# Cross-attention: context and K halves in two buffers each, projections in another order of steps, later weights asked for in the last group but one

## The reference

```python
x = x + xattn(layernorm(x), ctx, Wq, Wk, Wv, Wo)   # 16 heads of 16, ctx 32 x 256 x 256, no mask, no scale
x = x + attn(layernorm(x), wq, wk, wv, wo)         # 16 heads of 64, causal
x = x + ffn(layernorm(x), ...)                     # 256 -> 1024 -> 256, exact gelu, int8 weights, int16 activations
# xattn: q, k, v = split_heads(x @ Wq, ctx @ Wk, ctx @ Wv); softmax(q k^T) v; @ Wo
```

## Time and profile before

| | us |
|---|---|
| median of 3 runs | 672.53 |
| lowest and highest run | 670.81, 673.95 |
| span of the profiled execution | 669.4 |
| PE (matmul) busy | 608.3 (91%) |
| VectorE (DVE), ScalarE (ACT), GpSimd (POOL) busy | 469.9, 388.8, 197.3 |

### The profile page before, as it was taken

The page is one execution under the profiler, slowest core; times in us unless marked ns, Lnnn a source line. Parts: engine busy times, 40 slices in busy tenths (PEclk is TensorE's granted clock), DMA queues, the critical chain, the costliest instruction groups (busy, mean ns, idle before and its releaser), DMA issues. The chain is left out here.

```text
span 669.4 us, 18523 instructions
## 1 busy us (share of the span) xinstructions
PE 608.3 (91%) x6772; PEld 520.5 (78%) x6796; DVE 469.9 (70%) x989; ACT 388.8 (58%) x1017; POOL 197.3 (29%) x308
## 2 busy tenths in 40 slices
PE   6788799999999899979998999999999999788997
PEld 3577788888989788865887898888888897644597
DVE  4376867878787677875789847575756656467797
ACT  3386767888888687874351515242424333357895
POOL 4736234545454544400020303030312111250000
PEclk9899989999999899999999999999999999899999
DMA  7888958585857586720300000000000000000012
GB/s 252 184 236 215 269 143 208 139 211 139 210 136 186 117 199 146 171 52 3 125 2 1 2 1 0 0 0 0 0 0 0 2 1 2 9 3 0 1 43 84
DMA packets 35597, 58.44 MB, mean 87 GB/s; under 512 B 6912, under 2 KB 15232, under 8 KB 35552
## 3 DMA queue, kind: packets, MB, share of 16 engines
q1 hardware_dynamic: 25008, 36.85, 21.8%
q0 software_dynamic: 5952, 12.20, 7.5%
q10 hardware_dynamic: 4592, 8.78, 4.8%
HBM read 17.96 MB, written 2.10 MB: 30 GB/s over the span
## 5 line engine op out<-in xcount | busy, mean ns | idle before, releaser
L573 ACT ACTIVATE Pr<-pS,nmax 128x256 f32<-128x256 f32 x256 | 119.8, 480 | 25.1 <-DVE nmax L677 24.5
L677 DVE TENSOR_REDUCE nmax<-pS 128x2 f32<-128x512 f32 x128 | 87.4, 683 | 35.6 <-PE pS L416 35.2
L899 POOL TENSOR_TENSOR a_Pr<-a_Pr,a_rinv 128x512 f32<-128x512 f32 x32 | 32.8, 1045 | 185.8 <-DVE a_rinv L1188 185.8
L426 PE MATMUL pT<-ident,Pr 128*128 128x128 f32 x512 | 78.5, 276 | 0.1
L416 PE MATMUL pS<-Kst,Qst 96*128 96x256 f32 x256 | 57.2, 305 | 21.6 <-DMA Kst<-KSl 16.6
L341 POOL TENSOR_TENSOR CSl<-CT,CSh 128x1024 fp32r<-128x1024 f32 x15 | 35.3, 2355 | 114.5 <-ACT CSh L566 114.5
L271 POOL DMA_DIRECT2D Qst<-QSh x124 | 62.0, 503 | 13.7 <-DVE QSl L649 6.9
L416 PEld LDWEIGHTS pS<-Kst,Qst 96*128 96x128 f32 x256 | 41.5, 192 | 30.2 <-issue 15.2
L1068 ACT ACTIVATE a_Pr<-a_Pr 128x512 f32<-128x512 f32 x32 | 20.2, 631 | 76.0 <-DVE a_Pr L1180 76.0
L426 PEld LDWEIGHTS pT<-ident,Pr 128*128 128x128 f32 x512 | 60.1, 142 | 0.8 <-ACT Pr L573 0.4
L573 ACT ACTIVATION_READ_ACCUMULATOR Pr<-pS,nmax 128x1 f32 x256 | 54.1, 211 | 0.0
(11 more groups left out here) (269 smaller groups left out, 1925.1 us busy)
## 6 DMA issues: line engine op xcount, KB each, us to landing
Kst<-KSh SPq DMA_DIRECT2D x126, 128.0 KB, 2.9
CT<-ctxT ACTq DMA_DIRECT2D x16, 512.0 KB, 5.6
Kst<-KSl SPq DMA_DIRECT2D x63, 128.0 KB, 3.7
Qst<-QSh POOLq DMA_DIRECT2D x124, 64.0 KB, 2.1
Qst<-QSl POOLq DMA_DIRECT2D x62, 64.0 KB, 2.1
X<-x SPq DMA_DIRECT2D x4, 512.0 KB, 9.0
out<-X SPq DMA_DIRECT2D x8, 256.0 KB, 2.2
raw<-awq SPq DMA_DIRECT2D x1, 1024.0 KB, 5.9
```

The lines of the kernel that those rows point to most:

```text
L426: last = pe.transpose(pT[s % 2][:, t, k, :], Pr[s % 2][:, t, P * k:P * k + P], ident[:, :])
L573: act.activation(Pr[c % 2][:, t, :], pS[c % 2][:, t, :], ACT.Exp, bias=nmax[c % 2][:, t:t + 1], accum_out=rsum[par][:, c // 4, 2 * (c % 4) ...
L677: dve.tensor_reduce(nmax[s % 2][:, :], pS[s % 2][:, :, :], AX.X, ALU.max, negate=True).then_inc(maxed, 1)
L899: pool.tensor_tensor(rows, rows, rinv[s][:, :].unsqueeze(2).to_broadcast([P, 8, SQ]), ALU.mult).then_inc(weighted, 1)
```

## The change

It has five parts. `CS` gets two buffers by the pair's parity. `KS` gets two as well; the second lies in the tensor WO_ints, which the third layer fills later. In the table of events, K of the next even pair moves from steps 6 and 7 to 2 and 3, V of this odd pair from 2 and 3 to 6 and 7, V of the next even pair from 9 and 10 to 10 and 14, and K of the next odd pair from 13 and 14 to 11 and 12. ScalarE's `ctx_high` and `load_ctx` move with it. Before the first group, K of pair 1 comes ahead of the first two scores, with 10 and 4 spare matmuls for 22 and 12. The self-attention's weights are asked for in group 6.

```diff
-        CS = [sb(f"CS{s}", [P, KC, PK], F32R) for s in "hl"]
+        CS = [[sb(f"CS{b}{s}", [P, KC, PK], F32R) for s in "hl"] for b in range(2)]
...
-        KS = [sb(f"KS{s}", [P, 2, PK], F32R) for s in "hl"]
+        KS = [[sb(f"KS{s}", [P, 2, PK], F32R) for s in "hl"],
+              [ints[:, 4 * s:4 * s + 4, :].rearrange("p (a b) d -> p a (b d)", a=2) for s in range(2)]]
...
+        EVENTS = {0: (0, "X", 2, 0), 2: (1, "K", 2, 0), 3: (2, "K", 2, 1), 4: (3, "Q", 2, 0), 6: (4, "V", 1, 0),
+                  7: (5, "V", 1, 1), 10: (6, "V", 2, 0), 11: (7, "K", 3, 0), 12: (8, "K", 3, 1), 14: (9, "V", 2, 1)}
...
             def body(i, last):
-                p = 2 * i
-                first = isinstance(i, int) and i == 0
+                late = isinstance(i, int) and i == QUADS - 2
                 if not last:
-                    if first:
+                    restack_k(sp, 0, EV0 + EV * i + 2, CHUNKS * (2 * i + 1))
+                    if late:
                         load_later(0)
-                    restack_k(sp, 0, EV0 + EV * i + 5, CHUNKS * (p + 1))
-                    if first:
-                        load_later(1)
-                        load_later(2)
-                    restack_k(sp, 1, EV0 + EV * i + 9, CHUNKS * (p + 2))
-                    if first:
-                        load_later(3)
+                    restack_k(sp, 1, EV0 + EV * i + 8, CHUNKS * (2 * i + 2))
+                    if late:
+                        for m in range(1, 4):
+                            load_later(m)
...
-            spare(22)
+            spare(10)
             for r, (kind, ahead, part) in enumerate(AHEAD):
...
-                if r == 6:
-                    spare(12)
-                    score(0, 0)
-                    score(0, 1)
-                project(r, r, kind, part, ahead, 3)
+                project(r, r, kind, part, ahead, ahead % 2, 3)
+            spare(4)
+            score(0, 0)
+            score(0, 1)
...
             for r, (kind, ahead, part) in enumerate(AHEAD):
-                if r == 6:
-                    ctx_high(1, 1, 6)
-                    exps(0, 0)
                 high(r, r, kind, ahead, part, None)
                 if r == 2:
                     restack_k(act, 0, 1, 0, (3,))
+                    ctx_high(1, 1, 0)
+                    load_ctx(2, 0, 1)
+            load_ctx(3, 1, 2)
+            exps(0, 0)
+            ctx_high(0, 2, 6)
...
-                    if s == 0 and not last:
-                        load_ctx(2 * i + 2, 0, 2 * i + 1)
-                    if s == 2 and not last:
-                        load_ctx(2 * i + 3, 1, 2 * i + 2)
+                    if s == 3 and two_ahead(i):
+                        load_ctx(2 * i + 4, 0, 2 * i + 3)
+                    if s == 13 and two_ahead(i):
+                        load_ctx(2 * i + 5, 1, 2 * i + 4)
...
-                    if s == 4 and not last:
-                        ctx_high(0, i + 2, EV0 + EV * i + 3)
-                    if s == 11 and not last:
-                        ctx_high(1, i + 2, EV0 + EV * i + 8)
+                    if s == 8 and not last:
+                        ctx_high(1, i + 2, EV0 + EV * i + 6)
+                    if s == 15 and two_ahead(i):
+                        ctx_high(0, i + 3, EV0 + EV * i + 10)
```

More of the change, by code:

```diff
@@ L377, in weights, with project @@
                 return [(W[HI][:, m, k, cols], W[LO][:, m, k, cols]) for k in range(KC)]
-            def project(r, k_, kind, part, pair, q_needs=None):
+            def project(r, k_, kind, part, pair, b, q_needs=None):
                 after(pe, lo, r - 1)
@@ L396, in project @@
                     pe.wait_ge(ctx_lo, pair + 1)
-                    last = split_matmul(pe, bank[:, :], weights(1, slice(P * part, P * part + P)), parts(CS))
+                    last = split_matmul(pe, bank[:, :], weights(1, slice(P * part, P * part + P)), parts(CS[b]))
                 else:
@@ L437, in weigh @@
                     first = isinstance(i, int) and i == 0
-                    pe.wait_ge(lo, EV0 + EV * i + (2 if last else 3) if par else 6 if first else EV0 + EV * i - 2)
+                    pe.wait_ge(lo, EV0 + EV * i + (2 if last else 6) if par else 6 if first else EV0 + EV * i)
                     after(pe, merged, 2 * i + par)
@@ L494, in body @@
                         r, k, kind, ahead, part = event(i, s, last)
-                        project(r, k, kind, part, 2 * i + ahead, r - 1)
+                        project(r, k, kind, part, 2 * i + ahead, ahead % 2, r - 1)
                     if s == 11 or (s == 3 and not first):
@@ L559, in high @@
                 else:
-                    dst, how, kw = target(HI, kind, part)
+                    dst, how, kw = target(HI, kind, part, ahead % 2)
                     act.activation(dst, bank[:, :].rearrange(how, **kw) if kw else bank[:, :], ACT.Copy).then_inc(hi, 1)
@@ L653, in low @@
                 else:
-                    dst, how, kw = target(LO, kind, part)
-                    high = f32(target(HI, kind, part)[0])
+                    dst, how, kw = target(LO, kind, part, ahead % 2)
+                    high = f32(target(HI, kind, part, ahead % 2)[0])
                     dve.tensor_tensor(dst, bank[:, :].rearrange(how, **kw) if kw else bank[:, :], high,
```

30 lines of the change are left out of this document (13 added, 17 removed).

## The result

| | before | after |
|---|---|---|
| median of 4 runs each, us (same chip) | 672.25 | 661.44 (659.37 to 661.87) |
| ratio, 95% interval | | 0.9837, 0.9804 to 0.9871 |
| profiled execution: span, us | 669.4 | 657.6 |
| its own time, us | | 659.37 |
| cross-attention ends (first `a_pO` matmul), us | 311.38 | 299.89 |

The kernel is 1.6% faster. The forecast was 658 us in a range of 649 to 667, with 0.85 on faster. Sign and size were right, and so was the mechanism of the gain, the waits for Kst and `On`; the new limit that it named, GpSimd at step 11, hardly shows. The median is 3.4 us above the forecast, half a per cent. One term of the sum, group 5, was further off than that, by 3.9 us, and the steady groups were 1.9 us off the other way; the two partly cancel.

The account below looks back on a forecast made before the run. TensorE was taken to set the pace, its idle time being what groups can give back. Span 669.4 - 17.4 (groups) + 3.4 (start) = 655.4 us, plus 3.1 from span to median: 658 us, range 649 to 667.

Parts of the forecast that it names:

- Waits for Kst: Cross-attention scores at steps 6 and 14: earlier K projections remove the waits, 16.6 us in ten before.
- cover of 3.8 us: Kst[1] restack: landed 40.2 us after the group's start, wanted at 44.0, so 3.8 us to spare.
- rival 3: Q and Kst[1] restacks collide with a context load from 28 to 37 us into each group: 662 us, chance 0.08.
- `On` and the weights: Step 12's wait for `On` is covered, 0.83 us less a group; moving the later weights to group 6 costed at 0.
- Steady group: A cross-attention group without its Kst wait: 32.45 us, less 0.83 for `On`, plus 1.3 of new waiting, 32.9 us.
- wait of 1.3 us for CSl at step 11: TensorE's K projection waits 1.3 us for GpSimd's low context part, seen 22.6 us into the group; bounds 0 and 3.
- Rival 2: CSl is ready in time at step 11, so the 1.3 us wait is gone in seven groups: 649 us, chance 0.11.
- group 5 4.1: Group 5, 36.97 us with a 2.96 us Kst wait and slow clock, was to give back 4.1 us.
- nothing to spare: CSl at step 2: GpSimd needs 8.35 us of some 8.5 available; no wait, costed at 0, 0.3 a group for range.
- Rival 4: Slower than before: the CSl wait nears 3 us and the clock falls in each of seven groups: 681 us, chance 0.09.
- The start: Before group 0: K of pair 1 ahead of the scores puts the third score at 36.1 us for 32.80; 3.4 lost.
- Rival 1: TensorE's clock stays low into group 0, 5 us of work at half rate: +2.5, 661 us, chance 0.18.

Follow-up runs that it names:

- Experiment 4: The changed kernel with one KS instead of two, K of each parity waiting for the other restack: 686.12 us, ratio 1.0228 to the kernel before.
- experiment 1: The kernel before with only the four later weights' loads moved from group 0 to group 6: 665.71 us, ratio 0.9908.
- experiment 2: The changed kernel with the later weights asked for in group 0 again: 659.73 us, ratio 0.9832 to the kernel before.
- experiment 8: The changed kernel with nine of the twelve DMAs of each Qst[0] restack on SyncE, GpSimd issuing 123: 653.66 us, ratio 0.9755 to the kernel before.
- experiment 12: The changed kernel with nine DMAs per Qst[0] restack on SyncE and the old start, pair 2's context load kept early: 652.5 us, ratio 0.9710.
- experiment 5: The changed kernel with the old start (22 and 12 spare matmuls, first two scores ahead of K of pair 1): 657.81 us, ratio 0.9802.
- experiment 10: The changed kernel with nine DMAs per Qst[0] restack on SyncE and the old start, pair 2's context load beside the Q restack: 654.74 us, 0.9740.
- experiment 3: The changed kernel with 20 more spare matmuls ahead of K of pair 1 at the start: 656.30 us, ratio 0.9762 to the kernel before.
- experiment 9: The changed kernel run again unaltered, on another chip: 661.12 us, ratio 0.9838 to the kernel before.
- experiment 6: The changed kernel with the first Qst[1] restack, twelve DMAs, issued by SyncE instead of GpSimd: 659.26 us, ratio 0.9828 to the kernel before.
- experiment 7: The kernel before with the first Qst[1] restack, twelve DMAs, issued by SyncE instead of GpSimd: 671.0 us, ratio 0.9993.
- experiment 11: The changed kernel with nine DMAs per Qst[0] restack on SyncE and more spare matmuls at the start (22, 20, 8): 654.49 us, ratio 0.9739.

## Why the prediction was right, and where it was not

**Waits for Kst, right.** All but 0.22 us went. The restack of Kst[1] was to start 28.7 us into the group and starts 28.4 in:

```profile
130.94 9.85 SPq L281 DMA_DIRECT2D Kst<-WO_ints  x12
```

Its issue takes 9.85 us rather than 8.3, beside the Q restack, and it lands at 145.14, 14.2 us after its first issue where 11.5 was taken; the score that needs it starts at 146.15. Of the cover of 3.8 us 1.0 is left. So rival 3 cost no time, but its mechanism, restacks that slow each other, is there, and larger than the 12.8 us that it reckoned with. Experiment 4 shows that the new order needs the second buffer; whether the buffers would do it without the new order no run shows.

**`On` and the weights, right,** the latter only together with the new order (experiments 1 and 2).

**Steady group, 32.5 and not 32.9.** The mis-sized term is the wait of 1.3 us for CSl at step 11. GpSimd's side was right to 0.3 us. TensorE's side was not: it was put at 21.3 into the group (21.4 by the sum's own terms) and came at 22.3. The sum counted no new small waits, and there are 0.42 for the exponentials behind the moved context copy and 0.22 at step 7; the rest of the 0.9 stands in no single wait. So the wait for CSl is 0.18 us where 1.3 was forecast, and with the two earlier ones it makes 0.82. The prediction called itself wrong "if step 11 waits 3 us or none": on this term that is what happened (no wait there is over 0.3 us in any group), although the total came out. The prediction moved ScalarE's context copy to step 8 and asked only when its result is ready, not what stands behind it on ScalarE. Rival 2, CSl in time, came nearer to what happened at this step, but not its price: experiment 8 takes 4.4 us of issue (9 DMAs of 0.49) from in front of it and gives 0.09 us a group.

**Group 5, the failed step.** The term "group 5 4.1" was taken from the length of the group and its Kst wait, as if it were of the same kind as the others. It gave 0.2. The row that would have told stood in GpSimd's queue at 206.27, 2.59 us with "issue" as the releaser, ahead of the very restack whose neighbour was late. The prediction read the SP queue for Kst[1] and GpSimd's for group 2, and not why group 5 differs from group 2 with the same program. It also wrote "no wait, but nothing to spare" for CSl at step 2 and costed it at 0 with 0.3 a group for the range; where nothing is to spare, any delay on that queue goes straight through, and there was one of 2.9 us. Rival 4 named this mechanism, CSl late by nearly 3 us with the clock falling behind it, but in seven groups instead of one, and at step 11. That the forecast was still met is in part luck: an error of 3.9 us here against one of 1.9 us in the other groups.

**The start, right in size, its cause told too simply.** The third score came at 36.30 for 36.1. The terms: CSl used at 28.8 for 28.0, K 4.2 us for 5.0, spares 0.7 for 0.9, scores and exponentials 2.6 for 2.2. The size holds over the executions, at 35.05 to 36.80 against 32.80. The prediction put it down to the order of K and the scores. Two things cost here. One is that order: in experiments 8 and 12, whose first restack on SyncE begins within 0.03 us of each other and which both have the load early, the third score comes at 35.18 and 32.14. The other is a context load beside the first Q restack: it draws out the restack by 0.9 to 1.3 us (experiments 5 and 10 against 12), and in both traces that have it the clock fell behind the wait of the first scores. The size of this second part rests on one trace of each kernel, and the ratios of experiments 10 and 12 don't separate it. The change itself has the load early and pays for the order alone.

**Rival 1** happened in the profiled execution, and in those of experiments 3 and 4, but not in four others with the same start. The clock there was 0.61 and 0.53 from 38 to 42 us, after idle times of 1.80 and 0.40 us; group 0 was 0.4 us longer for it (32.94 against 32.52 in experiment 9), not 2.5. The row for "what would show it", a clock of 1.00 to the end of the stage, was missed on this and on group 5. The Trainium skill, "TensorE: Matmul & The Clock Gate", section "A second HAM failure mode: psum-queue depth-cycling", describes such swings between short gaps; here the same program shows the fall in one execution and not in the next.

**The sum.** Group by group the forecast was 17.4 and the trace has 15.1: 3.9 short in group 5, 1.9 over in groups 1 to 4 and 6, 0.3 short in groups 0 and 7. With 0.2 more lost at the start and 0.3 gained in the rest the span is 657.6 for 655.4. On top, 3.1 us were added to get from span to median. The execution's own time is 1.8 us above its span; the other 1.3 stood for a profiled execution of before that was quicker than its median. That held again (659.37 against 661.44), a little more so. 2.2 from the span, 0.7 from this last step and 0.5 from rounding 658.5 down make the 3.4.

## To carry to other kernels

Of groups that run the same program, ask of each one that is longer what is different in *its* rows, on every queue, before counting its excess as a gain; a stall labelled "issue" is a cause of its own and survives a new order. Where the new order leaves "nothing to spare" on a queue, the longest stall seen on that queue is the price to put on it, once. And undo parts both alone and together: here the weights' move was worth 6 us alone and nothing on top of the rest. The old start brought nothing alone in its trace, and with one load in its place 3.1 us at the start of group 0 and 1.6 at the stage's end, which the times of the runs do not separate from chance.

## What the runs showed of the hardware

**GpSimd's DMA queue stalls once, by count.** In ten of the fourteen traces (the thirteen kernels, the changed one twice), those that issue more than 128 DMAs from GpSimd in this stage (before, after, experiments 1 to 7 and 9), the engine stops for 2.6 to 2.9 us behind the 128th; it moved by one restack when twelve DMAs were taken from in front of it (experiments 6 and 7), and the four kernels with 123 DMAs (8, 10, 11, 12) have none. All these DMAs are of 64 KB, so a count of DMAs can't be told from one of bytes or packets:

```profile
q0 software_dynamic: 5952, 12.20, 7.8%
```

This queue's bytes are those of GpSimd's 186 DMAs, 32 packets each, so that 4096 packets lie ahead of the stall. It isn't a wait for transfers still under way: in the changed kernel the 127th and 128th DMA landed at 196.98 and 197.54, and the 129th was issued at 198.87. The kernels issue at most 186, so whether it comes again is open, and so is what the queue does in that time. SyncE issues its own 128th DMA at 170.57 in the changed kernel and the 129th at 171.26, without a gap. The name "issue" alone is not enough to find the stall: in experiments 1, 5 and 12 the first DMA of a restack in group 0 carries it too (1.15, 4.06 and 4.06 us), where every other restack waits for a score or for Q.

**The same idle time is not always followed by the lower clock.** TensorE idled for 2.82 us ahead of 206.18 in the changed kernel and the clock was 0.50 behind it; it idled for 2.81 us ahead of 225.60 in experiment 6 and it stayed:

```profile
224.00:226.00 2.00, 0.40 (x2) 0.39 (x3) 0.01 (x1) 0.14 (x2) 1.46 (x1) 1.00 0.00 0
226.00:228.00 2.00, 2.00 (x15) 1.73 (x14) 0.41 (x2) 0.00 (x0) 0.00 (x0) 1.00 0.00 0
```

That is the difference between group 5's 36.76 and 35.49. Nor is it the place: of the six traces that idle 2.82 to 2.84 us at step 2 of group 5, five show the fall, and in that of experiment 4 the clock stayed at 1.00 (230 to 234 us). In experiment 12 TensorE idled for 3.33 us at the start and the clock stayed at 1.00 as well; after 4.18 and 4.66 us, in experiments 5 and 10, it fell. And in the changed kernel's group 0 idle times of 1.80 and 0.40 us were followed by it, with the same idle times and no fall in experiments 2, 6, 8 and 9. An idle time near 3 us is thus a risk, of some 1.3 to 1.4 us in group 5, and not a fixed price.
